# Exponentials of two score steps in one ScalarE instruction, with a ring of six probability slots

## The reference

```
logits = jnp.einsum('bihd,bjhd->bhij', q, k) * scale + pos_bias[None]
attn = jax.nn.softmax(logits, axis=-1)
out = jnp.einsum('bhij,bjhd->bihd', attn, v).reshape(B, S, D)
```

## Time and profile before

| | |
|---|---|
| median of three runs | 1292.52 us |
| profiled execution, its own time | 1297.87 us |
| its span, first to last instruction | 1296.0 us |
| mean granted TensorE clock | 0.956 |
| busy in the span: PE | 91% |
| DVE (VectorE) | 66% |
| ACT (ScalarE) | 61% |
| POOL (GpSimd) | 60% |

### The profile page before, as it was taken

The page is one execution under the profiler, slowest core; times in us unless marked ns, Lnnn a source line. Parts: engine busy times, 40 slices in busy tenths (PEclk is TensorE's granted clock), DMA queues, the critical chain, the costliest instruction groups (busy, mean ns, idle before and its releaser), DMA issues.

```text
span 1296.0 us, 28185 instructions
## 1 busy us (share of the span) xinstructions
PE 1180.9 (91%) x10747; PEld 683.0 (53%) x10747; DVE 859.6 (66%) x1468; ACT 794.3 (61%) x947; POOL 772.5 (60%) x515
## 2 busy tenths in 40 slices
PE   7998899999999999999899999539999999999980
PEld 3444233333333333333345453329999999999980
DVE  4454899999889998997547887724444444444445
ACT  4554899999999999998366667302222222222224
POOL 1233688788887888887246887734445444444433
PEclk9999899999999999999799999669999999999995
DMA  7699554495559554462267862977777777777748
GB/s 224 201 326 285 221 75 75 76 264 91 87 86 271 84 83 75 80 128 78 82 170 193 207 189 99 177 245 234 236 245 235 235 236 244 242 240 244 236 111 263
DMA packets 134207, 232.50 MB, mean 179 GB/s; under 512 B 31601, under 2 KB 80534, under 8 KB 133750
## 3 DMA queue, kind: packets, MB, share of 16 engines
q1 hardware_dynamic: 102416, 178.08, 46.9%
q0 software_dynamic: 25024, 39.74, 16.4%
q10 hardware_dynamic: 6630, 12.82, 3.5%
HBM read 103.91 MB, written 52.76 MB: 121 GB/s over the span
## 4 chain that ended last, share of the span: by engine, by line
PE 67%; DVE 15%; issue 5%; POOL 5%; ACT 5%; DMA 3%; ACTq 0%; SPq 0%; DVEq 0%; POOLq 0%
PE xp_ps_h L2371 20%; PE xp_ps_y L2383 9%; PE sa_sum L668 9%; PE sa_o L682 9%; DVE sa_probs L714 8%; PE sa_factor L668 4%; PE qp_ps L302 4%; PE qp_ps L329 2%; POOL sorted L1086 2%; ACT sa_probs L738 1%; PE xp_ps_x L2360 1%; DVE sa_o_out L702 1%; PE cb_misc L1240 1%; ACT fi_rows L2497 1%; PE cb_l L1255 1%
## 5 line engine op out<-in xcount | busy, mean ns | idle before, releaser
L714 DVE TENSOR_TENSOR sa_probs<-sa_sum,sa_strips 128x1024 f32<-128x1024 f32 x352 | 413.2, 1219 | 45.5 <-PE sa_sum L668 43.4
L758 POOL TENSOR_TENSOR sa_probs<-sa_probs,sa_factors 128x1024 f32<-128x1024 f32 x160 | 383.7, 2398 | 99.0 <-ACT sa_probs L732 99.0
L738 ACT ACTIVATE sa_probs<-sa_probs 128x1024 f32<-128x1024 f32 (+1 forms) x256 | 343.0, 1385 | 0.2 <-DVE sa_probs L714 0.2
L2371 PEld LDWEIGHTS xp_ps_h<-arena,big 128*128 128x128 f32 x2272 | 266.3, 193 | 5.1 <-ACT arena L2401 1.6
L2371 PE MATMUL xp_ps_h<-arena,big 128*128 128x128 f32 x2272 | 266.9, 276 | 0.9 <-ACT arena L2401 0.9
L682 PE MATMUL sa_o<-sa_probs,sa_v 128*17 128x512 f32 x2048 | 265.6, 594 | 0.8 <-POOL sa_probs L758 0.6
L2339 POOL DMA_INDIRECT y_sum<-stage,xp_place_of x71 | 113.1, 1593 | 192.2 <-DMA y_sum<-stage,xp_place_of 96.2
L668 PE MATMUL sa_sum<-sa_qk 97*32 97x512 bf16 x2816 | 201.6, 382 | 16.1 <-DVE sa_probs L714 7.0
L668 PEld LDWEIGHTS sa_sum<-sa_qk 97*32 97x32 bf16 x2816 | 63.2, 95 | 234.2 <-DVE sa_probs L714 130.9
L732 ACT ACTIVATE sa_probs<-sa_factor 128x1024 f32<-128x1024 f32 x160 | 164.5, 1028 | 4.9 <-PE sa_factor L668 3.4
L2383 PE MATMUL xp_ps_y<-big,arena 128*128 x568 | 134.5, 380 | 1.3 <-DVE arena L2438 1.3
(11 more groups left out here) (238 smaller groups left out, 1283.7 us busy)
## 6 DMA issues: line engine op xcount, KB each, us to landing
big<-big SPq DMA_DIRECT2D x142, 512.0 KB
sa_strips<-line SPq DMA_DIRECT2D x3, 3840.0 KB, 18.8
sa_qk<-qstack SPq DMA_DIRECT2D x84, 128.0 KB
sa_qk<-kstack SPq DMA_DIRECT2D x84, 128.0 KB
oT<-sa_o_out SPq DMA_DIRECT2D x32, 256.0 KB, 2.4
kstack<-qp_parts SPq DMA_DIRECT2D x48, 128.0 KB, 3.9
qstack<-qp_parts SPq DMA_DIRECT2D x48, 128.0 KB
sa_factors<-factor_line SPq DMA_DIRECT2D x3, 1920.0 KB, 23.1
```

The lines of the kernel that those rows point to most:

```text
L714: nc.vector.tensor_tensor(probs[s % RING][:, 2 * half:2 * half + 2, :], ps_sum[sums_before(s, half) % 2][:, :, :], strips[hg % 2][:, 2 * h ...
L738: nc.scalar.activation(probs[s % RING][:, 0:heads, :], probs[s % RING][:, 0:heads, :], ACT.Exp, scale=0.25).then_inc(exp_done, 1)
L758: nc.gpsimd.tensor_tensor(probs[s % RING][:, 2:4, :], probs[s % RING][:, 2:4, :], factors[hg % 2][:, :, c1 - CH:c1][:, :, ::-1], ALU.mult) ...
L2371: last = nc.tensor.matmul(ps_h[parity % 2][:, n, m * P:(m + 1) * P], w_now[s % WRING][:, n, k, m * P:(m + 1) * P], xT[parity % 2][:, k, :] ...
```

## The change

The exponential of the sums is taken for two steps at once. In even steps s ScalarE issues one instruction for the sums of steps s - 2 and s - 1. For this the ring becomes one tensor of six slots (`RING` 6, `LAG` 5), and in an even factor step the two halves are stored swapped, so that the sums of an even step and the following odd one lie side by side (`at`). `BY_FACTOR` changes from (0, 2, 3, 5, 6) to (0, 1, 3, 4, 6). The output copy moves from `jt` 3 to `jt` 5. The bias rows are loaded into two tensors, the second one shorter. VectorE and ScalarE also wait for `keys_shifted` once at the start.

```
-BY_FACTOR = (0, 2, 3, 5, 6)
+BY_FACTOR = (0, 1, 3, 4, 6)
...
-        RING, LAG, KEYS = 4, 3, 32
+        RING, LAG, KEYS = 6, 5, 32
...
-        probs = [sb(f"probs{i}", [P, HPG, CH]) for i in range(RING)]
+        probs = sb("probs", [P, RING * HPG, CH])
+
+        def at(s, half):
+
+            swapped = is_factor(s, 1) and s % 2 == 0
+            return HPG * (s % RING) + 2 * (half ^ swapped)
...
             def values(s):
...
-                pe.wait_ge(exp_done, s + 1)
+                pe.wait_ge(exp_done, s // 2 + 1)
...
-                if jt == 3 and s > JT:
+                if jt == 5 and s > JT:
                     copy_out(s // JT - 1)
...
             def exp_of_sums(s):
-                heads = 2 if is_factor(s, 1) else HPG
-                act.wait_ge(added, sums_before(s, 0) + heads // 2)
-                nc.scalar.activation(probs[s % RING][:, 0:heads, :], probs[s % RING][:, 0:heads, :], ACT.Exp,
-                                     scale=0.25).then_inc(exp_done, 1)
+                first, end = at(s, 0), at(s + 1, 0) + (2 if is_factor(s + 1, 1) else HPG)
+                act.wait_ge(added, sums_before(s + 2, 0))
+                nc.scalar.activation(probs[:, first:end, :], probs[:, first:end, :], ACT.Exp, scale=0.25).then_inc(exp_done, 1)
 
             act.wait_ge(front_stored, 1)
+            act.wait_ge(keys_shifted, 2)
             for s in range(NSTEP + 1):
                 if s < NSTEP and is_factor(s, 1):
                     exp_of_scores(s)
-                if s >= 1:
-                    exp_of_sums(s - 1)
+                if s >= 2 and s % 2 == 0:
+                    exp_of_sums(s - 2)
...
+def load_second_strips(eng, io, strips, hg, h=0, n=2):
+
+    lines = bass.AP(io["line"].tensor, (hg * HPG + 2 + h) * 2 * S + SUM_FROM, [[1, P], [2 * S, n], [1, STRIP - SUM_FROM]])
+    return eng.dma_start(strips[1][:, h:h + n, :], lines)
```

More of the change, by code:

```diff
@@ L34 @@
 STRIP = S + (JT - 1) * P
+SUM_FROM, FACTOR_TO = 2 * P, STRIP - P
 RES, TAPS, NF = 128, 101, 4
@@ L72, in load_strips, with load_first_strips @@
     return eng.dma_start(strips[:, h:h + n, :], lines)
+def load_first_strips(eng, io, strips, hg, h=0, n=2):
+    lines = bass.AP(io["line"].tensor, (hg * HPG + h) * 2 * S, [[1, P], [2 * S, n], [1, STRIP]])
+    return eng.dma_start(strips[0][:, h:h + n, :], lines)
+def load_second_strips(eng, io, strips, hg, h=0, n=2):
+    lines = bass.AP(io["line"].tensor, (hg * HPG + 2 + h) * 2 * S + SUM_FROM, [[1, P], [2 * S, n], [1, STRIP - SUM_FROM]])
+    return eng.dma_start(strips[1][:, h:h + n, :], lines)
 def load_factors(eng, io, factors, hg, h=0, n=2):
-    lines = bass.AP(io["factor_line"].tensor, (hg * HPG + 2 + h) * 2 * S, [[1, P], [2 * S, n], [1, STRIP]])
+    lines = bass.AP(io["factor_line"].tensor, (hg * HPG + 2 + h) * 2 * S, [[1, P], [2 * S, n], [1, FACTOR_TO]])
     return eng.dma_start(factors[:, h:h + n, :], lines)
@@ L130, in attention_space @@
         "v": [sb(f"v{i}", [P, JT, HPG * VW]) for i in range(2)],
-        "strips": sb("strips0", [P, HPG, STRIP]),
-        "factors": sb("factors0", [P, 2, STRIP]),
+        "strips": [sb("strips0", [P, 2, STRIP]), sb("late_strips0", [P, 2, STRIP - SUM_FROM])],
+        "factors": sb("factors0", [P, 2, FACTOR_TO]),
         "loaded": [sem(f"loaded{i}") for i in range(2)],
@@ L390, in strip @@
                     act.wait_ge(line_stored, 16)
-                load_strips(act, io, sa["strips"], 0, h, 1).then_inc(sa["strips_loaded"][0], 16)
+                (load_first_strips, load_second_strips)[h // 2](act, io, sa["strips"], 0, h % 2, 1
+                                                                ).then_inc(sa["strips_loaded"][0], 16)
             def factor(h):
@@ L666, in scores @@
                         for c in range(P // KEYS):
-                            at = jt * P + c * KEYS
-                            last = nc.tensor.matmul(into[c * KEYS:(c + 1) * KEYS, a, :], k[m % 2][:, h, at:at + KEYS],
+                            key = jt * P + c * KEYS
+                            last = nc.tensor.matmul(into[c * KEYS:(c + 1) * KEYS, a, :], k[m % 2][:, h, key:key + KEYS],
                                                     q[m % 2][:, h, ih * CH:(ih + 1) * CH], start=True, stop=True)
@@ L682, in values @@
                     last = nc.tensor.matmul(ps_o[n % 2][32 * h:32 * h + VW, :], v[m % 2][:, jt, VW * h:VW * (h + 1)],
-                                            probs[s % RING][:, h, :], start=(jt == 0), stop=(jt == JT - 1))
+                                            probs[:, at(s, h // 2) + h % 2, :], start=(jt == 0), stop=(jt == JT - 1))
                 last.then_inc(pv_done, 1)
@@ L696, in _ @@
             dve.wait_ge(front_stored, 1)
+            dve.wait_ge(keys_shifted, 2)
             def copy_out(n):
@@ L707, in _ @@
                 if s % (B * STEPS) == 0:
-                    dve.wait_ge(strips_loaded[hg % 2], (16 * HPG if hg % 2 == 0 else 16) + 16 * (hg // 2))
+                    dve.wait_ge(strips_loaded[hg % 2], (16 * HPG if hg % 2 == 0 else 32) + 32 * (hg // 2))
                 if s >= RING:
@@ L713, in _ @@
                         dve.wait_ge(sum_scores, sums_before(s, half) + 1)
-                        nc.vector.tensor_tensor(probs[s % RING][:, 2 * half:2 * half + 2, :],
+                        end = c1 - SUM_FROM * half
+                        nc.vector.tensor_tensor(probs[:, at(s, half):at(s, half) + 2, :],
                                                 ps_sum[sums_before(s, half) % 2][:, :, :],
-                                                strips[hg % 2][:, 2 * half:2 * half + 2, c1 - CH:c1][:, :, ::-1],
+                                                strips[hg % 2][half][:, :, end - CH:end][:, :, ::-1],
                                                 ALU.add).then_inc(added, 1)
-                if jt == 3 and s > JT:
+                if jt == 5 and s > JT:
                     copy_out(s // JT - 1)
```

11 lines of the change are left out of this document (6 added, 5 removed).

## The result

The changed kernel takes 1334.53 us (median of 4 runs, 1330.59 to 1336.65) against 1293.1 us (4 runs of the kernel before, with them on the same chip). The ratio is 1.0293, 95% interval 1.0269 to 1.0318: slower by 2.9%, 41 us. The forecast was 1328 us.

What follows compares the result with a forecast made beforehand. Self-attention was taken as bounded equally by ScalarE and by PE with VectorE through two `sa_sum` tiles. 31 groups x 1.13 = 35.0 us, plus 0.3 for start and end, on a 1292.5 median gave 1328 us; own range 1316 to 1340.

Steps and rivals of the forecast that it cites:

- The other bound: Self-attention: PE and VectorE, handing over two `sa_sum` tiles, need 14.78 us per group of eight, the same as ScalarE's beat.
- S of 3072 elements: ScalarE's merged exponential of sums: 2.64 us from start to start, bounds 1.79 to 2.84.
- F4 1.74 behind F3: ScalarE's factor-half exponential of `jt` 4 starts 1.74 us after that of `jt` 3, not 0.91, through the one `sa_factor` tile.
- Idle ahead of F0: ScalarE waits some 0.6 us in each group before the factor-half exponential of `jt` 0.
- The table of the chain: Event starts followed over PE, VectorE and ScalarE through one group: closes at 15.94 us, 1.13 above the mean of 14.81.
- Ring and lag at nothing: Products waiting for a pair's exponential, with ring of six and lag of five, have 4 us of cover; costed at nothing.
- the sentence that ScalarE idles 0.83 us in every group: ScalarE, between the neighbouring factor exponentials of `jt` 3 and 4: idle 0.83 us per group, raising its beat to 15.09.
- only the round trip costs: Rival: only the `sa_factor` round trip between `jt` 3 and 4 costs, VectorE catches up; beat 15.09, +9, 1301 us; chance 0.10.
- The copy costs its 0.60: The output copy, moved behind a step of two sums, adds its 0.60 us to the chain; before it took nothing extra.
- The start: Start of the self-attention stage: PE has no products for five steps, up to 2.6 us gained.
- The end: End of the self-attention stage, from the last factor exponential to the last copy: about 8.8 us, 2.9 later than before.
- The prediction's bounds (6, 8 and 3): Uncertainty in us: merged exponential's length +6, latencies at five places 8 either way, start and end 3; own range 1316 to 1340.

Runs made afterwards that it cites:

- the three kernels with halved work: The kernel before, with exponentials of sums, VectorE's additions, or both over half the columns; beats 14.77, 14.70, 13.84 us, ratios 0.999, 0.997, 0.976.
- split_between_3_and_4: Changed kernel with the copy at `jt` 4 and step 2's exponential of sums issued between the factor exponentials of `jt` 3 and 4; beat 15.68 us, ratio 1.024.
- unmerged_after: Changed kernel with one exponential of sums per step again, copy still at `jt` 5; beat 15.16 us, ratio 1.015.

## Why the prediction was right, point by point

- **The other bound** (14.78 from PE and the two `sa_sum` tiles): right, by the three kernels with halved work.
- **S of 3072 elements, 2.64 from start to start:** 2.66 (406.89 to 409.55), mean length 2.758 for the 2.77 forecast.
- **F4 1.74 behind F3:** 1.75 (412.25 to 414.00). Idle ahead of F0 forecast 0.6, measured 0.47.
- **The table of the chain, 15.94 a group:** 15.92, over the very events of the table. The copy and the five additions of `jt` 5 to 7 follow each other without a gap from 415.36 on.
- **Ring and lag at nothing:** right; in the middle of the stage PE's products wait for nothing. At the end they do.
- **What the wait between F3 and F4 means:** the sentence that ScalarE idles 0.83 us in every group counts from start to start, and so counted it is 1.75 - 0.91 = 0.84 (the row's 0.72 counts from the end of F3). Its use as a price was not tested by the forecast, and split_between_3_and_4 shows it to be no part of the loss. The table had it right without saying so: it runs from F3 to PE's scores for F4 and never through F4. So the rival "only the round trip costs" named a sum of ScalarE's that did not bind in any of the runs.
- **The copy costs its 0.60:** mis-sized as a price of the place. Moved to `jt` 4 it gives back 0.25: it still takes part in the loop there (above), and other waits take up the rest.
- **The size, 35 against 41 us.** The loop itself was sized well; the terms beside it were not. From F6 of the first group to F6 of the last it is 37.6 more (147.48 to 644.21, 496.73 us): 31 x 1.11 = 34.4 for the beat and the rest for the two long groups, which the forecast did not see: the reciprocal was not followed though the copy moved next to it. The start was to give 2.6 and gives 0.2 (F6 13.51 behind the first addition, before 13.68). The end was to cost 2.9 and costs 3.7 (9.61 from F6 to the last copy, before 5.90). Why the start gave so little was not followed. The prediction's bounds (6, 8 and 3) would add up to 1317 to 1345, not 1316 to 1340; the measured time lies within both. The last rows of the stage, ACT and DVE:

```profile
644.21 1.02 ACT L754 ACTIVATE sa_probs<-sa_factor 128x1024 f32<-128x1024 f32 x1
...
649.01 2.77 ACT L760 ACTIVATE sa_probs<-sa_probs 128x3072 f32<-128x3072 f32 x1 [1.13 <-DVE sa_probs L736]
```

```profile
653.82 0.69 DVE L723 COPY sa_o_out<-sa_o 128x512 f32<-128x512 f32 x1 [4.83 <-PE sa_o L702]
```

The last S waits 1.13 us for an addition, behind the reciprocal of that group.

## What to carry to other kernels

Before work is taken off the fullest engine, follow what the others would do without it: here PE and VectorE had the same beat through two tiles, and a full ScalarE was no sign of a gain. When several engines hand one tile back and forth, write the loop down event by event; an idle time that the profile names need not be in it, and an experiment that removes the idle time but not the loop changes nothing. Merging instructions moves work in time as well as saving its fixed cost: put the long pieces where the partner has slack, the short ones between close hand-overs.

## What was not expected of the hardware

One stall lowered TensorE's clock in two places, and a stall of much the same size did not in a third. In the first of the long groups of the changed kernel PE waited 1.84 us for an addition. It was busy for 0.66 of 2.50 us, and the granted clock then was 0.54 over 3.50 us (the lower level, 1.2 GHz, for most of it); a product took 1.66 us there instead of 1.03. So part of the 2.78 us of that group is the clock. Stretches of the changed kernel from 578 us:

```profile
578.00:580.50 2.50, 0.66 (x16) 0.25 (x16) 2.50 (x3) 2.50 (x1) 2.37 (x1) 1.00 0.09 23
580.50:584.00 3.50, 3.50 (x32) 1.08 (x28) 2.64 (x3) 0.24 (x2) 0.00 (x0) 0.54 0.20 77
```

In the group of 20.47 us of unmerged_after PE waited 2.89 us, and the clock was 0.50 from 560 to 566 us. But in that run's group of 16.76 us PE waited 2.11 us, longer than the 1.84 above, and the clock stayed at 1.00:

```profile
593.00:595.50 2.50, 0.48 (x12) 0.00 (x0) 1.99 (x3) 2.09 (x2) 2.13 (x1) 1.00 0.98 181
595.50:599.00 3.50, 3.41 (x48) 1.19 (x48) 3.43 (x4) 2.08 (x3) 0.23 (x1) 1.00 0.67 231
```

So the length of one wait does not tell by itself whether the clock falls. The idle times of PE of 0.5 to 0.6 us that come in every group did not lower it: it is 1.00 from 386 to 504 us.
